# A two-layer convolution, attention and experts kernel: gathers kept to two under way, sampling work spread differently, loads in another order

## The reference, cut to what matters here

```python
out = v00 * (1 - wx) * (1 - wy) + v01 * wx * (1 - wy) + v10 * (1 - wx) * wy + v11 * wx * wy
...
qh = q.reshape(Bb, Hh, Ww, G, HC).transpose(0, 3, 1, 2, 4).reshape(Bb, G, P, HC) * scale
attn = jnp.einsum('bgpc,bgpkc->bgpk', qh, k)
attn = jax.nn.softmax(attn, axis=-1)
out = jnp.einsum('bgpk,bgpkc->bgpc', attn, v)
...
x = x + _L0_conv_ref(_gn(x), ...)
```

## Time and profile before

| | us |
|---|---|
| median of 3 runs (lowest, highest) | 9661.08 (9647.11, 9673.49) |
| the profiled execution | 9657.97 |
| its span, from the first to the last instruction | 9656.2 |
| PE / DVE / ACT / POOL busy | 7727.8 / 5175.6 / 3767.1 / 5070.2 |
| gathers (L727) busy, 4608 of them | 4812.6 |
| granted TensorE clock, mean | 0.894 |

### The profile page before, as it was taken

The page is one execution under the profiler, slowest core; times in us unless marked ns, Lnnn a source line. Parts: engine busy times, 40 slices in busy tenths (PEclk is TensorE's granted clock), DMA queues, the critical chain, the costliest instruction groups (busy, mean ns, idle before and its releaser), DMA issues. The chain is left out here.

```text
span 9656.2 us, 96652 instructions
## 1 busy us (share of the span) xinstructions
PE 7727.8 (80%) x31522; PEld 4168.2 (43%) x31522; DVE 5175.6 (54%) x10029; ACT 3767.1 (39%) x5495; POOL 5070.2 (53%) x4864
## 2 busy tenths in 40 slices
PE   7637776645894799869999977997999799989699
PEld 3623333433442344434444433443444344435466
DVE  6543335545564566656666555665653466634233
ACT  2101102201462266525666533662666255541232
POOL 1057777667777777777777777777730000001322
PEclk9868888867897799988999988997999799999799
DMA  3844335666543544454444355445430311115221
GB/s 129 289 150 137 120 119 178 213 217 211 161 138 112 175 138 144 130 179 126 138 139 146 119 176 180 142 129 178 137 101 28 94 46 46 40 45 157 81 73 54
DMA packets 658546, 1283.59 MB, mean 133 GB/s; under 512 B 189043, under 2 KB 398218, under 8 KB 643408
## 3 DMA queue, kind: packets, MB, share of 16 engines
q0 software_dynamic: 234240, 639.57, 21.2%
q1 hardware_dynamic: 405392, 562.58, 19.5%
q10 hardware_dynamic: 18432, 75.51, 2.0%
HBM read 1003.44 MB, written 278.91 MB: 133 GB/s over the span
## 5 line engine op out<-in xcount | busy, mean ns | idle before, releaser
L727 POOL DMA_INDIRECT sa_slot<-s_table,sa_rec x4608 | 4812.6, 1044 | 2279.2 <-issue 1382.9
L1704 DVE CUSTOM_DVE_ANT_0 a_above<-a_late,a_above 128x512 f32<-128x512 f32 x1600 | 1101.6, 689 | 1436.5 <-PE a_late L1556 1321.5
L1636 ACT ACTIVATE a_p<-a_s 128x1024 f32<-128x1024 f32 x1600 | 1628.6, 1020 | 124.4 <-PE a_s L1594 122.6
L1611 PE MATMUL a_ctx<-a_p,a_v 128*64 128x512 f32 x6400 | 1577.3, 614 | 85.0 <-issue 84.5
L1645 ACT ACTIVATE a_above<-a_diff 128x512 f32<-128x512 f32 x1600 | 956.6, 598 | 1648.2 <-PE a_diff L1544 1379.7
L769 DVE TENSOR_TENSOR sa_slot<-sa_slot,sa_q 128x1152 f32<-128x1152 f32 x512 | 694.0, 1355 | 1021.6 <-DMA sa_slot<-s_table,sa_rec 1005.1
L1594 PE MATMUL a_s<-a_q,a_k 98*128 98x512 f32 x3200 | 1047.3, 411 | 3.2 <-ACT a_p L1636 3.2
L878 PE MATMUL sa_sums<-keep_ident,sa_vals 128*128 128x128 f32 x4608 | 681.3, 297 | 420.9 <-DVE sa_vals L821 420.9
L1556 PE MATMUL a_late<-a_k,a_q 96*128 96x512 f32 x1600 | 815.2, 510 | 168.0 <-DVE a_pair_max L1704 164.6
L1544 PE MATMUL a_diff<-a_kd,a_q 96*128 96x512 f32 x1600 | 725.5, 453 | 194.8 <-DMA a_q<-s_q 157.6
L878 PEld LDWEIGHTS sa_sums<-keep_ident,sa_vals 128*128 128x128 f32 x4608 | 609.5, 155 | 518.6 <-DVE sa_vals L821 439.4
(11 more groups left out here) (280 smaller groups left out, 8089.3 us busy)
## 6 DMA issues: line engine op xcount, KB each, us to landing
sa_slot<-s_table,sa_rec POOLq DMA_INDIRECT x4608, 3.1
s_table<-t_rows ACTq DMA_DIRECT2D x64, 1024.0 KB, 7.7
a_q<-s_q SPq DMA_DIRECT2D x480, 128.0 KB, 3.5
s_part<-a_o SPq DMA_DIRECT2D x160, 256.0 KB, 2.4
t_qwin<-s_dwq SPq DMA_DIRECT2D x64, 512.0 KB, 6.9
t_kvwin<-s_dwkv SPq DMA_DIRECT2D x64, 386.0 KB, 10.3
a_kd<-s_kd SPq DMA_DIRECT2D x384, 64.0 KB, 3.4
a_o<-s_part SPq DMA_DIRECT2D x96, 256.0 KB, 3.6
```

The source lines that it names most:

```text
L727: pool.indirect_dma_start(out=self.slot[g][:, k, :, :, :].rearrange("p c a n -> p (c a n)"), out_offset=None, in_=self.s["table"][n // TIL ...
L1611: mm = pe.matmul(self.ps_ctx[i * 2 * HD:(i + 1) * 2 * HD, :], self.v_and_ones(run.head, kb), self.p[slot % P_SLOTS][:, i * CHUNK:(i + 1) * ...
L1636: act.activation(self.p[slot % P_SLOTS][:, :], self.ps_s[slot % 2], ACT.Exp, scale=float(HD) ** -0.5).then_inc(self.exped, 1)
L1704: dve.tensor_tensor_reduce(above, self.ps_late, above, 1.0, LOWEST, ALU.add, ALU.max, self.pair_max[:, t, j:j + 1]).then_inc(self.late_got, 1)
```

## The change

Six edits, in one step:

1. **Gathers.** Each group has two semaphores, used in turn ("lanes"). A gather is issued only when the gather two before it has landed, across groups too. EARLY is gone. `q_times_k` waits for both lanes.
2. **Projection.** A projection takes 25 pieces in place of 33, and spreads them over its 6 steps rather than 6 of 8 shares.
3. **Attention.** The last 5 slots of an attention stage bring no new pieces. With edits 2 and 3 the piece numbers at the stages' ends become: 282; 307; 358; 522; 547; 703; projection (0,2) 762 then 787; 1048; 1073; 1438; 1463; 1514; 1539; 1695; projection (1,2) 1722 then 1747; 1932.
4. **Loads at the border** to an attention stage: the first `kd`, then the first `q`, then the first `k`, then the other `kd`, then the rest.
5. **Head.** SP loads x and the weights of `stage_maps` first, then those of `prepare_weights`. PE multiplies the taps ahead of its first wait of `stage_maps`, and waits for `diag_made` later. The taps are copied by ACT ahead of its own work, not by DVE.
6. **Clearing of `buf`.** POOL clears its tiles of `stage_maps` first, then issues the 16 fills, after x has landed.

```diff
+UNDER_WAY = 2
+LAST_SLOTS = 5
-PROJECT_PIECES = 33
+PROJECT_PIECES = 25
-EARLY = 7
...
-    @block.sync
-    def _(sp):
+    def load(sp):
         sp.dma_start(pconv[:, :, :, :], d["pconv"]).then_inc(loaded, 16)
...
+    def clear(pool, maps_in):
         pool.memset(offset_w.taps[:, :, :], 0.0).then_inc(zeroed, 1)
         pool.memset(zeros[:, :], 0.0).then_inc(blank, 1)
 
         pool.wait_ge(blank, 1)
+        pool.wait_ge(maps_in, 16 * CH)
         for i in range(FILLS):
...
+    def copy(act):
+        act.wait_ge(zeroed, 1)
         for tap in range(TAPS):
-            dve.wait_ge(made, tap + 1)
-            dve.tensor_copy(offset_w.taps[0:CQ, tap, :], banks[tap % 2][0:CQ, 0:OFFS]).then_inc(copied, 1)
+            act.wait_ge(made, tap + 1)
+            act.activation(offset_w.taps[0:CQ, tap, :], banks[tap % 2][0:CQ, 0:OFFS], ACT.Copy).then_inc(copied, 1)
...
             sp.dma_start(keep.ident[:, :], d["ident"]).then_inc(ident_in, 16)
+            load_taps(sp)
+            store_taps(sp)
...
-            end_of_weights(pool)
+            clear(pool, xt_in)
 
         @block.tensor
         def _(pe):
+            multiply_taps(pe)
             pe.wait_ge(wts, 80)
-            pe.wait_ge(diag_made, MT * TAPS)
...
                 pe.wait_ge(xn_ready, b + 1)
+                pe.wait_ge(diag_made, MT * TAPS)
...
+            copy_taps(act)
             act.wait_ge(wts, 80)
...
-        self.gathered = [r.sem(f"gathered{g}") for g in range(G)]
-        self.gathered_late = [r.sem(f"gathered_late{g}") for g in range(G)]
+        self.landed = [[r.sem(f"landed{g}_{lane}") for lane in range(UNDER_WAY)] for g in range(G)]
...
+    def in_lane(self, lane):
+        return len(range(lane, K, UNDER_WAY))
+
     def gather(self, pool, n, g):
...
-        if G * n + g > 0:
-            before = G * n + g - 1
-            pool.wait_ge(self.gathered[before % G], 16 * EARLY * (before // G + 1))
         for k in range(K):
+            if k >= UNDER_WAY:
+                lane = k % UNDER_WAY
+                pool.wait_ge(self.landed[g][lane], 16 * (self.in_lane(lane) * n + k // UNDER_WAY))
+            elif G * n + g > 0:
+                before = G * n + g - 1
+                lane = (K - UNDER_WAY + k) % UNDER_WAY
+                pool.wait_ge(self.landed[before % G][lane], 16 * self.in_lane(lane) * (before // G + 1))
             pool.indirect_dma_start(
...
-            ).then_inc(self.gathered[g] if k < EARLY else self.gathered_late[g], 16)
+            ).then_inc(self.landed[g][k % UNDER_WAY], 16)
...
-        dve.wait_ge(self.gathered[g], 16 * EARLY * (n + 1))
-        dve.wait_ge(self.gathered_late[g], 16 * (K - EARLY) * (n + 1))
+        for lane in range(UNDER_WAY):
+            dve.wait_ge(self.landed[g][lane], 16 * self.in_lane(lane) * (n + 1))
...
         def pieces(j):
-            return begin + (upto - begin) * (j + 1) // (STEPS + 2)
+            return begin + (upto - begin) * min(j + 1, STEPS) // STEPS
...
     def first_loads(self, sp):
-        for n in range(min(self.QR, len(self.runs))):
+        self.load_kd(sp, 0, 0)
+        self.load_q(sp, 0)
+        self.load_k(sp, 0)
+        for g in range(1, self.c + 1):
+            self.load_kd(sp, 0, g)
+        for n in range(1, min(self.QR, len(self.runs))):
             if n < self.KR:
                 self.load_k(sp, n)
-            if n == 0:
-                for g in range(self.c + 1):
-                    self.load_kd(sp, 0, g)
             self.load_q(sp, n)
...
         def pieces(slot):
 
+            slot = min(slot, at.slots - LAST_SLOTS)
             return begin + (4 * (min(slot, 0) + at.lead) + 7 * max(slot, 0)) * Sampling.PIECES // (7 * TILE_SLOTS)
```

More of the change, by code:

```diff
@@ L155, in sem, with prepare_weights @@
         return sem
-def prepare_weights(nc, stack, block, d, s, keep):
+def prepare_weights(nc, stack, d, s, keep):
     r = Room(nc, stack, "w")
@@ L168, in prepare_weights, with store @@
     blank, blanked, taps_out = r.sem("blank"), r.sem("blanked"), r.sem("taps_out")
-    @block.sync
-    def _(sp):
+    def load(sp):
         sp.dma_start(pconv[:, :, :, :], d["pconv"]).then_inc(loaded, 16)
         sp.dma_start(offset_w.off_w[:, :, :], d["off_wT"].rearrange("(h p) n -> p h n", p=P)).then_inc(loaded, 16)
+    def store(sp):
         sp.wait_ge(copied, TAPS + 1)
@@ L176, in _ @@
         sp.wait_ge(taps_out, 16)
-    @block.gpsimd
-    def _(pool):
+    def clear(pool, maps_in):
         pool.memset(offset_w.taps[:, :, :], 0.0).then_inc(zeroed, 1)
@@ L183, in _, with multiply @@
         pool.wait_ge(blank, 1)
+        pool.wait_ge(maps_in, 16 * CH)
         for i in range(FILLS):
             pool.dma_start(s["buf"].rearrange("(i p r) n -> i p (r n)", i=FILLS, p=P)[i], zeros[:, :]).then_inc(blanked, 16)
-    @block.tensor
-    def _(pe):
+        pool.wait_ge(blanked, 16 * FILLS)
+    def multiply(pe):
         pe.wait_ge(loaded, 32)
@@ L198, in _ @@
         pe.wait_ge(copied, TAPS)
-    @block.vector
-    def _(dve):
-        dve.wait_ge(zeroed, 1)
+    def copy(act):
+        act.wait_ge(zeroed, 1)
         for tap in range(TAPS):
-            dve.wait_ge(made, tap + 1)
-            dve.tensor_copy(offset_w.taps[0:CQ, tap, :], banks[tap % 2][0:CQ, 0:OFFS]).then_inc(copied, 1)
[L206 to L212, removed]
+            act.wait_ge(made, tap + 1)
+            act.activation(offset_w.taps[0:CQ, tap, :], banks[tap % 2][0:CQ, 0:OFFS], ACT.Copy).then_inc(copied, 1)
+        act.wait_ge(loaded, 32)
+        act.activation(offset_w.taps[CQ:P, TAPS // 2, :], offset_w.off_w[CQ:P, 0, :], ACT.Copy).then_inc(copied, 1)
+    return banks, load, store, clear, multiply, copy
 def stage_maps(nc, d, s, keep):
@@ L248, in stage_maps @@
         block = stack.enter_context(nc.Block())
-        ps_d, end_of_weights = prepare_weights(nc, stack, block, d, s, keep)
+        ps_d, load_taps, store_taps, clear, multiply_taps, copy_taps = prepare_weights(nc, stack, d, s, keep)
         Q_COPIES = (3, 1)
```

## The result

The changed kernel takes **11842.45 us** (median of 4 runs, 11835.41 to 11847.16), the kernel before 9667.28 us beside it. The ratio is 1.2254 with a 95% interval of 1.2232 to 1.2275: 22.5% slower. The forecast was 11732 us in a range of 10700 to 12550.

The account below looks back on a forecast made before the run. POOL's gather chain was taken to bound the kernel, between a head and a tail: 9656 us of span + 2180 (chain) - 86 (tail) - 20 (head) = 11730, plus 2 around the span: 11732 us, range 10700 to 12550.

Parts of the forecast that it names:

- The chain sets the time: POOL's 4608 gathers, first to last start, are held only by their own pace: 6596.0 us, predicted 2180 us more.
- The pitch is (landing + d) / 2: Time per gather step; d, landing to POOL's next start, is 0.31 us in the mean: 1.905 us, from 1.432.
- The rival by which dispatch costs 0.80 each time: Each new wait of POOL's gathers costs 0.80 us, not 0.25: pitch 2.15, 12861 us; chance 0.1.
- The mean landing: Time from a gather's start to its landing: 3.68 us in the kernel before, 3.5 with bursts scaled for the slower pitch.
- the quiet median alone would decide: Rival for gather landings: bursts of other transfers vanish, pitch 1.705, 10811 us; chance 0.2.
- No shorter landing with fewer under way: Gathers' landing doesn't shrink with fewer under way; the rival that it does, not slower, gave 9552 us, chance 0.04.
- The foreground has no slack: Attention stages run at the gathers' pace and can't swallow a slower chain; rival, growth partly hidden: 9700 to 10400 us, chance 0.04.
- The tail, -86 us: Last gather to the end, 2531 us: edits 2 and 3 move 37 attention slots under the chain, gaining 86 us.
- The head, -20 us: Before the first gather, 528.8 us: edits 5 and 6 start the first product near 62 us, gaining 20 us (0 to 40).
- The border loads: Edit 4 at attention stage starts: q issued about 20 us earlier over seven stages, beside the chain, so counted at nothing.

Follow-up runs that it names:

- the four runs: Edit 1 alone, the first of edits 2 to 6, the first of three under way, and one under way: 11953.63, 11851.33, 11481.84, 19215.16 us; kernel before there 11847 us.

## Why the prediction was right, step by step

**The chain sets the time.** Right for the slower chain. Edit 1 gives the whole loss, and head, chain and tail add up to the span in each run.

**The pitch is (landing + d) / 2.** Right as the mechanism. Predicted 1.905, measured 1.930. The size of d was right: 0.29 and 0.28 us in the two places shown. Over the changed kernel, by starts and semaphore events, it is 0.26 in the median for the gathers within a group and 0.76 for the first of a group, where 0.25 and 0.80 were predicted. As an equation between means it is too short, though: the mean landing of 3.43 and a d of 0.31 give 1.87, not 1.930. In 1208 of 4607 steps POOL did not stand and wait but went on at its free step, and the time of a long landing is not won back there. The rival by which dispatch costs 0.80 each time would have given 12861 us; it is out.

**The mean landing.** For the kernel before 3.68 was worked out, from how long POOL waited at the 128 borders where it did wait, and 3.71 is counted. For two under way 3.5 was predicted and 3.43 is counted: the bursts' part fell more than by 1.43/1.9. So there is some luck in 11732 against 11842. A landing taken 0.07 too long (160 us of chain) made up for over half of what the equation between means leaves out (some 260 us). That the quiet median alone would decide (10811 us) is out as well.

**No shorter landing with fewer under way.** Right for the median and the shortest, and shown at one: 3.0 and 2.7. The mean does fall, to 3.20. The Trainium skill's fit for a transfer from POOL's queue (DMA: Bandwidth & Descriptors, section Anatomy of one DMA, SWDGE path) gives 2.3 us for this size, as an estimate; the traces disagree, and no gather of any run was under 2.7.

**The foreground has no slack.** What was drawn from it held: with the slower chain the foreground waits for the chain, and the time grows by all that the chain grows. But the reason was too simple in the other direction. Where the chain is near its old pace, the foreground holds it up in turn: the pieces alone lengthen it by 107.5 us, and POOL's wait for DVE grows by 89. That is why edits 2 to 6 came 107 us over their forecast. It is no cause for three under way (POOL waits 20.7 us for DVE) and about half of it for four; there the landings were longer than those put into the rule.

**The tail, -86 us.** The size was right (-89), the meaning only half. From 9394.4 us on, 124 exponentials are left where 162 were the earlier trace rows, so 38 slots moved and 37 were predicted. I had written that these slots move under a chain that gains idle time, and that the gain would be lost where the chain isn't the bound. With the old chain it is lost (1.0001, 0.999 to 1.0012). With the slow chain, the run with the old pieces puts it at 52 us net, since the chain is 45 us longer with the moved slots; the +2297 us of the chain hold these 45, which the prediction counted at nothing.

**The head, -20 us.** The first product starts at 64.03, 18 us sooner than in the earlier trace rows, and 62 was expected. The first gather comes 27 us sooner than in the profiled execution of before. Over nine traces with the new head it starts at 494.9 to 513.8 us, and over five with the old one at 519.6 to 529.4, so the head's gain is 21 us in the mean. The statistics wait for POOL's clears, as worked out:

```profile
22.69 9.59 DVE L379 BATCH_NORM_STATS2 m_stats<-m_xt 128x6 f32<-128x512 f32 x16 [22.69 <-POOL m_outkv L290]
...
41.42 15.87 ACT L337 ACTIVATE m_diag<-keep_ident,m_dw 128x128 f32<-128x128 f32 x54
```

**The border loads.** Counted at nothing, and no run has them alone. The 317.4 us in 14 waits of the earlier trace rows are 157.6 us in 7 waits of PE: that view adds the weight load and the product of the same wait. The waits of PE for q, in before, with edits 2 and 3, and with edits 2 to 6:

```profile
PE a_diff L1544 <- DMA a_q<-s_q: 157.6, 7, 30.3
...
PE a_diff L1545 <- DMA a_q<-s_q: 156.1, 7, 26.8
...
PE a_diff L1548 <- DMA a_q<-s_q: 122.2, 7, 25.8
```

So these waits are 34 us shorter with the new loads, where at most 20 was worked out. The time doesn't show it: edits 2 to 6 give 0.25% (20 us by the medians), which the head's 21 us explain by themselves.

## What to carry to other kernels

A limit of n transfers under way turns a stream that is paced by its issue into one that is paced by its latency: the step becomes (landing + restart) / n wherever this is over the free step. Both numbers can be read from a trace before the limit is built, and the mean landing, long ones included, is nearer than the median. Near the free step even the mean is too short (1.87 against 1.930 here), and the mean landing itself changes with n; playing the landings through in order does better, if they are those of a like n. Where the stream and the rest of the kernel run at nearly one pace, read also what the rest takes by itself before promising a gain from a faster stream: here the loss followed the stream one to one, while the foreground alone bounds any gain: with half the gathers left out, the time fell by 6%.

## What the runs showed of the hardware that was not expected

**On one chip the kernel before takes 22.6% longer, and how much longer a kernel takes there depends on how many gathers it lets be under way.** On the chip of the four runs the kernel before takes 11846.73 us (13 runs, 11703.0 to 11899.0), edits 2 to 6 alone 11851, three under way 11482. Two under way (edit 1 alone) take 11954, and one takes 19215. Neither was run on another chip, but both are near what head, chain and tail give from the other traces; the largest difference is a tail of edit 1 alone that is 29 us longer than in before. So with two under way or fewer this chip shows little that is odd, and with more it loses about 2200 us (1550 with three). There the limit of two costs 1.2% (0.1 to 2.2), not 23%.

The trace of edits 2 to 6 on that chip shows where the time is. POOL's source line, then waits of DVE and ACT that no instruction explains, then an instance:

```profile
  DVE sa_vals L823: 2508.5, 112
...
DVE a_above L1708 <- remote: 739.9, 92, 26.1
...
ACT a_above L1649 <- remote: 858.4, 126, 25.2
...
4999.42 0.67 PE L1548 MATMUL a_diff<-a_kd,a_q 96*128 96x512 f32 x1
...
5004.14 0.60 ACT L1649 ACTIVATE a_above<-a_diff 128x512 f32<-128x512 f32 x1 [6.50 <-remote]
```

The chain isn't the bound there: POOL waits 2508.5 us for DVE, and POOL's free step is 1.25 us as everywhere. PE's product is recorded as ended at 5000.09, and the activation that waits only for it starts at 5004.14. In the semaphore events of that trace the product's update comes at 5004.12, four microseconds after the recorded end, and in between PE's records show further products starting, from 5000.02 on. Waits named "remote" appear in the two traces with more than two under way on that chip, and hardly in the others (20 us in one place of edit 1 alone). Whether the update is late or PE itself stood still can't be told from these traces, since ends of matmuls are modelled. Nor is it known whether it is the chip or its condition at that hour. No run of the kernel before was profiled there.

**Gathers' descriptors take longer beside DVE's products of two tensors, and not beside its reduction.** Counted from the starts and durations in the trace of before, 442 of the 506 gathers that start while DVE's product L769 runs took over 1.0 us (mean 1.43), and 279 of the 479 that start during its product L821 (mean 1.33). Of the 521 that start during its reduction L775 it is 2 (mean 0.95), and of the 3105 that start beside none of the three it is 58 (mean 0.95). The earlier trace rows has one of 1.66 among its neighbours. In the changed kernel it is 467 of 481, 294 of 380, 1 of 427 and 39 of 3320, and the mean of the first kind is 1.69, so the mean of all is 1.068 and not 1.044, although POOL idles between gathers there. The difference of 0.024 x 4608 = 111 us is small beside the 2297 us of the chain.
